# Layer-norm statistics of the feed-forward tiles moved from VectorE to two ScalarE passes, and one GpSimd instruction moved up

## The chip, the cores and the metric

The kernel runs on one core of one Trainium2 chip. The metric is device time in microseconds (us) of the whole program, the median of three runs. TensorE does the matmuls, VectorE (DVE), ScalarE (ACT) and GpSimd (POOL) the rest of the arithmetic, and SyncE (SP) issues the DMAs. Each engine runs its own queue in order; semaphores order the queues against each other.

## What is computed

A macaron block on x of 8 x 1024 rows of 256 columns: half a feed-forward, attention, half a feed-forward. The feed-forward quantizes its input and its hidden layer to four-bit values in blocks of 16:

```python
def fp4_quant_dequant(x):          # along the last axis, blocks of 16
    scale = jnp.maximum(jnp.max(jnp.abs(xb), axis=-1, keepdims=True) / 6.0, 1e-12)
    xn = xb / scale
    idx = jnp.searchsorted(_MID, jnp.abs(xn))
    q = _GRID[idx] * jnp.sign(xn) * scale

def ffn(x, w_gate, w_up, w_down):  # 256 -> 704 -> 256, each product on quantized operands
    h = silu(fp4_linear(x, w_gate)) * fp4_linear(x, w_up)
    return fp4_linear(h, w_down)

x = x + 0.5 * ffn(layernorm(x)); x = x + attention(layernorm(x)); x = x + 0.5 * ffn(layernorm(x))
```

The change touches the two layer norms ahead of the feed-forwards: mean and variance of each row of 256, then z = (x - mean) * rstd.

## The kernel before

All of x stays in SBUF as `xs`, 64 tiles of 128 rows x 256. `feed_forward(phase, ...)` runs twice, for phase 0 and 1, over the 64 tiles, one tile a step. It is a software pipeline written out by hand: each engine has a function `step(i, par)`, and `steps()` calls it for i from -6 to 63; the calls from 4 to 57 are a hardware loop of nine rounds of six steps, the others are written out. In step i an engine works on several tiles at different stages, and its queue is the order of the lines in `step`. A call `done(engine, name, i)` makes the engine wait until tile i of the named result is ready.

The stages of one tile, with the line of the profile: VectorE takes the statistics (`bn_stats` L712, `bn_aggr` L770); GpSimd makes eps_var (L824), rstd (L827) and shift = -mean * rstd (L786); ScalarE makes z (L919); VectorE takes the block maxima of z (L730) and of h (L735); GpSimd makes both scales, dscale (L840) and nscale (L851), for both at once; VectorE takes the reciprocal rec (L756); GpSimd multiplies z and h by it (v_z L793, v_h L857); ScalarE takes magnitudes (L907, L869) and VectorE rounds (L741, L675, L762, L681); GpSimd scales back (xq L818, hq L802). TensorE transposes xq (L987), ScalarE rounds the transposed tile to its high part (xT_hi L874) and VectorE makes the low part (xT_lo L704); the gate and up projections (L935) follow, then silu on ScalarE (L896) and the product h on VectorE (L720). For the hidden layer TensorE transposes hq (L951), ScalarE makes hT_hi (L880), VectorE hT_lo (L665), TensorE projects down (L942 to L945), and VectorE adds the result to `xs` (L670).

Orders within step i that matter here:

- TensorE: first bank of gate and up of tile i; transposes of tile i+1 (L987); the other banks; down projection of tile i-3, which waits for hT_lo; transposes of hq of tile i-2.
- ScalarE: silu; magnitude of v_h; magnitude of v_z; z of tile i+5, which waits for shift; xT_hi of tile i+2, which waits for the transposes; hT_hi of tile i-2.
- VectorE: hT_lo of i-3; bn_stats of i+6; h of i; the maxima; rounding; rec; rounding; xT_lo; bn_aggr of i+6.
- GpSimd: hq of i-2; xq of i+2; eps_var and rstd of i+5; dscale; shift of i+5; v_z of i+4, which waits for rec; nscale; v_h of i.

In the first steps weight preparation (`begin=weight_prep`, phase 0) or the output projection of the attention (`output_projection`, phase 1) runs between the steps, in parts, in the same queues. In the last six steps of a phase `ok(i + 6)` is false, so they issue no statistics, and the last five no z.

## Time and profile before

| | |
|---|---|
| median of three runs | 2042.45 us (2039.82 to 2044.85) |
| the profiled execution | 2039.79 us, its span 2038.0 us |
| busy share of the span | TensorE 97%, VectorE 90%, ScalarE 66%, GpSimd 53% |
| from 200 to 400 us (first feed-forward), busy of 200 us | TensorE 200.00, VectorE 196.52, ScalarE 101.25, GpSimd 175.85 |
| from 60 to 470 us | TensorE 405.86, VectorE 398.60, ScalarE 204.44, GpSimd 355.19 of 410 us |
| from 1612 to 2014 us | TensorE 402.00, VectorE 389.10, ScalarE 203.34, GpSimd 347.97 of 402 us |
| mean of one bn_stats (L712) and one bn_aggr (L770), 150 to 350 us | 0.417 us, 0.172 us |
| granted TensorE clock | 0.997 over the span, 1.00 in the feed-forwards |

The two feed-forwards take the first 480 us and the last 470 us; between them lies the attention, which the change leaves alone. The busy time of an engine is the sum of its instructions' records, overlaps counted once. Records of matmuls overlap, so a TensorE that is shown busy all the time may still lose time between the starts of its matmuls: the starts are what to read. VectorE, ScalarE and GpSimd rows show where an instruction began, how long it took, and in brackets how long its engine was idle before it and what ended that.

### The profile page before, as it was taken

To read this page: it belongs to the slowest core of one execution; us is meant where nothing else is said; L and a number is where in the kernel's file an instruction comes from. 1 tells how busy PE (TensorE), PEld (TensorE's weight loads), DVE (VectorE), ACT (ScalarE), POOL (GpSimd) and SP (SyncE) were. 2 spreads that over 40 slices of the span, in tenths; PEclk is the share of its full clock that TensorE was granted. 3 is DMA by queue.
4 is the path that set the end of the run, shared out by engine and by line. 5 is a ranking of instruction groups with operands and counts; after the bars stand their busy time and mean duration, and the time that the engine had idled before them with its cause. 6 is when DMAs were issued, how large, how long until landed. Compare 5 with 4: busy or idle time off the path is not lost. (4 is left out here: it accounts for less than half of the span.)

```text
span 2038.0 us, 44334 instructions
## 1 busy us (share of the span) xinstructions
PE 1974.5 (97%) x13254; PEld 1301.3 (64%) x13254; DVE 1838.7 (90%) x4649; ACT 1342.5 (66%) x2324; POOL 1088.6 (53%) x1785
## 2 busy tenths in 40 slices
PE   5999999998999999999999999999988899999999
PEld 3888888887887333333333333333328788888888
DVE  7999999998788899999999999999927799999997
ACT  5455555554887788888888888888883355545453
POOL 5788888885664222222222222212222688888885
PEclk9999999999999999999999999999999999999999
DMA  6000000001876555555555555555335000000000
GB/s 213 18 0 0 0 0 0 0 0 37 266 229 213 135 149 143 133 139 136 139 139 144 149 144 130 137 136 140 99 114 181 6 21 19 17 21 21 15 21 27
DMA packets 134842, 185.03 MB, mean 91 GB/s; under 512 B 24928, under 2 KB 76512, under 8 KB 134368
## 3 DMA queue, kind: packets, MB, share of 16 engines
q1 hardware_dynamic: 132000, 182.11, 31.8%
q8 instruction: 74, 1.21, 0.2%
q10 hardware_dynamic: 2688, 1.05, 0.2%
q14 instruction: 80, 0.66, 0.1%
HBM read 113.90 MB, written 85.98 MB: 98 GB/s over the span
## 5 line engine op out<-in xcount | busy, mean ns | idle before, releaser
L1939 POOL TENSOR_SCALAR_AFFINE_SELECT diag_scores<-diag_scores 128x256 f32<-128x256 f32 (+1 forms) x320 | 148.3, 463 | 672.8 <-ACT diag_scores L1908 664.9
L1404 DVE CUSTOM_DVE_ANT_0 gu_ps<-gu_ps,mask_qk 128x256 f32<-128x256 f32 (+3 forms) x690 | 340.5, 529 | 48.0 <-PE gu_ps L1389 40.3
L1389 PE MATMUL gu_ps<-k_stack,q_stack 96*128 96x512 bf16 (+3 forms) x1050 | 317.4, 334 | 2.7 <-DVE part_max L1409 0.5
L1843 PE MATMUL gu_ps<-probs,v_group 128*17 128x512 f32 (+3 forms) x3072 | 310.8, 492 | 3.2 <-ACT probs L1914 2.0
L935 PE MATMUL gu_ps<-wguT_hi,ffn_xT_hi 128*128 128x512 f32 (+1 forms) x768 | 309.1, 403 | 1.2 <-DVE ffn_xT_lo L704 1.2
L919 ACT ACTIVATE ffn_z<-xs,ffn_shift,ffn_rstd 128x256 f32 (+1 forms) x128 | 76.9, 601 | 321.7 <-POOL ffn_shift L786 321.6
L935 PE MATMUL gu_ps<-wguT_hi,ffn_xT_lo 128*128 128x512 f32 (+1 forms) x768 | 287.5, 374 | 0.0
L935 PE MATMUL gu_ps<-wguT_lo,ffn_xT_hi 128*128 128x512 f32 (+1 forms) x768 | 287.5, 374 | 0.0
L1910 ACT ACTIVATE probs<-hT_ps 128x256 f32<-128x256 f32 (+2 forms) x320 | 259.6, 811 | 13.7 <-PE hT_ps L1819 13.5
L1910 ACT ACTIVATE probs<-av_ps 128x256 f32<-128x256 f32 (+2 forms) x320 | 263.6, 824 | 0.1
L1389 PEld LDWEIGHTS gu_ps<-k_stack,q_stack 96*128 96x128 bf16 x1050 | 95.4, 97 | 256.0 <-DVE part_max L1404 183.3
L1409 DVE TENSOR_REDUCE part_max<-gu_ps 128x1 f32<-128x512 f32 x360 | 235.3, 683 | 4.3 <-PE gu_ps L1389 1.1
L1819 PE MATMUL hT_ps<-q_stack,k_stack 98*128 98x512 bf16 (+3 forms) x768 | 228.3, 327 | 2.6 <-DMA k_stack<-k_parts 2.1
L802 POOL TENSOR_TENSOR ffn_hq<-ffn_g_h,ffn_nscale 128x704 f32<-128x704 f32 (+1 forms) x256 | 210.4, 843 | 6.4 <-PE hT_ps L951 3.3
L1819 PE MATMUL av_ps<-q_stack,k_stack 98*128 98x512 bf16 (+3 forms) x768 | 191.0, 325 | 2.1 <-ACT probs L1910 1.9
L942 PE MATMUL xd_ps<-wdT_hi,ffn_hT_hi 128*128 128x256 f32 x630 | 186.2, 296 | 3.9 <-DVE ffn_hT_lo L665 3.9
L857 POOL TENSOR_TENSOR q_stack<-k_stack,ffn_rec 128x704 f32<-128x704 f32 x128 | 178.3, 1393 | 15.9 <-DVE ffn_rec L756 6.5
L942 PE MATMUL xd_ps<-wdT_hi,ffn_hT_lo 128*128 128x256 f32 x630 | 176.1, 280 | 0.0
L942 PE MATMUL xd_ps<-wdT_lo,ffn_hT_hi 128*128 128x256 f32 x630 | 176.0, 279 | 0.0
L1404 DVE CUSTOM_DVE_ANT_0 xd_ps<-xd_ps,mask_qk 128x128 f32<-128x128 f32 (+3 forms) x334 | 154.9, 493 | 6.1 <-PE xd_ps L1389 5.6
L935 PEld LDWEIGHTS gu_ps<-wguT_hi,ffn_xT_lo 128*128 128x128 f32 x768 | 144.1, 188 | 22.9
L935 PEld LDWEIGHTS gu_ps<-wguT_hi,ffn_xT_hi 128*128 128x128 f32 x768 | 144.6, 188 | 19.7 <-DVE ffn_xT_lo L704 1.9
(221 smaller groups left out, 4900.7 us busy)
## 6 DMA issues: line engine op xcount, KB each, us to landing
q_stack<-q_parts SPq DMA_DIRECT2D x192, 128.0 KB, 3.4
k_stack<-k_parts SPq DMA_DIRECT2D x192, 128.0 KB, 3.6
o_all<-o_sb SPq DMA_DIRECT2D x64, 256.0 KB
q_parts<-qkv_parts SPq DMA_DIRECT2D x32, 384.0 KB, 3.2
k_parts<-qkv_parts SPq DMA_DIRECT2D x32, 384.0 KB, 4.2
v_ones<-qkv_vst SPq DMA_DIRECT2D x16, 544.0 KB, 3.9
v_group<-v_ones SPq DMA_DIRECT2D x32, 272.0 KB, 4.3
xs<-in_L_attn_x SPq DMA_DIRECT2D x8, 1024.0 KB, 8.9
```

Of the source, the lines that this page charges most:

```text
L802: last = G.tensor_tensor(blocks(hq[:, to:to + n]), blocks(g_h[:, of:of + n]), spread(nscale[:, par, of // BLK:(of + n) // BLK]), ALU.mult)
L857: G.tensor_tensor(blocks(v_h[:, par, :]), blocks(h[:]), spread(rec[:, OF_H]), ALU.mult).then_inc(s["v_h"], 1)
L919: S.activation(z[:, 1 - par, :], x_tile(i + 5), ACT.Identity, bias=shift[:], scale=rstd[:]).then_inc(s["z"], 1)
L935: last = T.matmul(gu_ps[:, n, 0:cols.stop - cols.start], x[:, buf, k * P:(k + 1) * P], w[:, k, cols], start=k == 0 and m == 0, stop=k == K ...
L942: T.matmul(to, x[:, k * P:(k + 1) * P], w[:, k, :], start=k == 0 and n == 0, stop=False)
L1389: mm = T.matmul(out[:, e, :], qs[0:STACK, h0 + e, t * P:(t + 1) * P], ks[0:STACK, h0 + e, c * CHUNK:c * CHUNK + w], start=True, stop=True)
L1404: last = V.tensor_tensor_reduce(out=ps[:, e * w:(e + 1) * w], in0=ps[:, e * w:(e + 1) * w], in1=mask_qk[:, CHUNK - w:CHUNK], scale=1.0, sc ...
L1409: last = V.tensor_reduce(part_max[:, h0:h0 + per, t, c], ps[:, 0:per * w].rearrange("p (h w) -> p h w", h=per), AX.X, ALU.max)
L1819: mm = T.matmul(scores[pair][:, e, at:at + w], ks[0:STACK_MAX, h, t * P:(t + 1) * P], qs[0:STACK_MAX, h, (j + 1) * CHUNK - w:(j + 1) * CHUNK],
L1843: mm = T.matmul(o_ps[h * VPAD:h * VPAD + VCOLS, CHUNK - w:CHUNK], vs[:, t, h, :], probs[:, h // 2, i % 2, h % 2, at:at + w], start=first, ...
L1910: S.activation(probs[:, pair, i % 2, :, first:w], scores[pair][:, :, first:w], ACT.Exp, scale=DH ** -0.5).then_inc(s[pr], 1)
L1939: G.affine_select(out=block_of, in_=block_of, compare_op=ALU.is_ge, fill=MASKED, base=0, pattern=[[0, 2], [0, count], [1, P]], channel_mul ...
```

## The change

The statistics leave VectorE. `bn_stats` and `bn_aggr` go. ScalarE takes, for each tile, a copy with a summed output (`summed`, tile i+7 in step i) and a square of (x - mean) with a summed output (`squared`, tile i+6); both stand ahead of z of tile i+5. Their full outputs go to unused scratch columns. GpSimd gets one more instruction a step, `averaged`, which makes -mean of tile i+6 from the sum; eps_var becomes a multiply and an add on immediates, and shift a product of two columns. GpSimd's nscale is moved ahead of v_z. The written-out steps reach to 7 and start again at 56, so the loop has eight rounds in place of nine. ScalarE instead of VectorE waits for the loads of x and, in the output projection, for the finished rows.

```diff
@@ -540,6 +540,7 @@
...
                     S.activation(next_table[:, :], minus_half[:, :], ACT.Silu)
+                out_done(act, "resid", 2 if part < OUT_PARTS - 1 else OUT_CHUNKS - 1)
@@ -569,7 +570,7 @@
...
-        names = ("stats aggr eps rstd shift z amax_z amax_h dscale nscale rec v_h v_z av_h av_z u_h u_z g_h g_z hq xq "
+        names = ("total mean squares eps rstd shift z amax_z amax_h dscale nscale rec v_h v_z av_h av_z u_h u_z g_h g_z hq xq "
                  "xT xT_hi xT_lo gate up silu h hT hT_hi hT_lo down resid stored").split()
@@ -589,8 +590,8 @@
...
-                stats, aggr, eps_var, rstd, shift = (tmp("stats", [P, 6]), tmp("aggr", [P, 2]), tmp("eps_var", [P, 1]),
-                                                     tmp("rstd", [P, 1]), tmp("shift", [P, 1]))
+                total, squares, eps_var, rstd, shift = (tmp(n, [P, 1]) for n in ("total", "squares", "eps_var", "rstd", "shift"))
+                minus_mean = tmp("minus_mean", [P, 2])
                 xq = tmp("xq", [P, DIM])
@@ -613,6 +614,8 @@
...
+                scratch = [m[:, GROUP - 1, SEQ - DIM:SEQ] for m in second_stacks]
                 GU_BANKS = [slice(a, min(a + CHUNK, 2 * HIDDEN)) for a in range(0, 2 * HIDDEN, CHUNK)]
@@ -631,13 +634,17 @@
...
+                def first_step(i):
+                    return isinstance(i, int) and i == -AHEAD
                 def early(i, first=1):
...
-                    first, last, unroll = 4, TILES - 6, 6
+                    first, last, unroll = 8, TILES - 8, 6
                     for i in range(-AHEAD, first):
@@ -707,9 +714,6 @@
...
                                 hT_low(i - 3, hT, hT_flat)
-                            if ok(i + 6):
-                                done(dve, "aggr", i + 5)
-                                V.bn_stats(stats[:], x_tile(i + 6)).then_inc(s["stats"], 1)
                             if phase == 0 and early(i) and i == 1:
@@ -761,30 +765,25 @@
...
                                                        op0=ALU.max, op1=ALU.subtract).then_inc(s["g_z"], 1)
-                            if ok(i + 6):
-                                done(dve, "stats", i + 6)
-                                done(dve, "shift", i + 5)
                             if ok(i + 2) and not (early(i, -2) and i == -2):
                                 xT_low(i + 2, par)
-                            if ok(i + 6):
-                                V.bn_aggr(aggr[:], stats[:]).then_inc(s["aggr"], 1)
-                        def other_batches(i):
-                            if i is None:
-                                for b in range(2, BATCH):
-                                    dve.wait_ge(x_loaded[b], 16)
-                            elif (i + AHEAD) % SEQ_TILES == 0:
-                                dve.wait_ge(x_loaded[(i + AHEAD) // SEQ_TILES], 16)
-                        steps("vector", dve, step, finish, other_batches if phase == 0 else None)
+                        steps("vector", dve, step, finish)
...
                     def _(pool):
-                        def shifted(i):
+                        def shifted(i, par):
                             done(pool, "rstd", i)
                             pool.nop(nofuse=True)
-                            G.tensor_scalar(shift[:], aggr[:, 0:1], rstd[:], -1.0, ALU.mult,
-                                            ALU.mult).then_inc(s["shift"], 1)
+                            G.tensor_tensor(shift[:], minus_mean[:, par:par + 1], rstd[:], ALU.mult).then_inc(s["shift"], 1)
+                        def averaged(i, par):
+                            done(pool, "total", i)
+                            done(pool, "shift", i - 2)
+                            done(pool, "squares", i - 2)
+                            pool.nop(nofuse=True)
+                            G.tensor_scalar(minus_mean[:, par:par + 1], total[:], -1.0 / DIM, 0.0, ALU.mult,
+                                            ALU.add).then_inc(s["mean"], 1)
@@ -817,17 +816,22 @@
...
                                                 ALU.mult).then_inc(s["xq"], 1)
+                            if first_step(i):
+                                averaged(0, par)
+                            if ok(i + 6) and not first_step(i):
+                                averaged(i + 6, par)
                             if ok(i + 5):
-                                done(pool, "aggr", i + 5)
+                                done(pool, "squares", i + 5)
                                 done(pool, "z", i + 4)
-                                G.tensor_tensor(eps_var[:], aggr[:, 1:2], eps_tile[:, 0:1],
+                                pool.nop(nofuse=True)
+                                G.tensor_scalar(eps_var[:], squares[:], 1.0 / DIM, EPS, ALU.mult,
                                                 ALU.add).then_inc(s["eps"], 1)
...
                             if early(i, 0):
-                                shifted(i + 5)
+                                shifted(i + 5, 1 - par)
                             if early(i):
@@ -840,9 +844,7 @@
...
                             if ok(i + 5) and not early(i, 0):
-                                shifted(i + 5)
-                            if ok(i + 4) and not early(i, 0):
-                                over_scale_z(i, par)
+                                shifted(i + 5, 1 - par)
                             if ok(i) or ok(i + 4):
@@ -850,6 +852,8 @@
...
                                                 ALU.mult, ALU.min).then_inc(s["nscale"], 1)
+                            if ok(i + 4) and not early(i, 0):
+                                over_scale_z(i, par)
                             if ok(i):
@@ -884,6 +888,18 @@
...
                             S.copy(hT_end[0][:], hT_end_ps).then_inc(s["hT_hi"], 1)
+                        def summed(i):
+                            done(act, "mean", i - 1)
+                            act.nop(nofuse=True)
+                            S.activation(scratch[0], x_tile(i), ACT.Copy, accum_out=total[:]).then_inc(s["total"], 1)
+                        def squared(i, par):
+                            done(act, "mean", i)
+                            done(act, "eps", i - 1)
+                            act.nop(nofuse=True)
+                            S.activation(scratch[1], x_tile(i), ACT.Square, bias=minus_mean[:, par:par + 1],
+                                         accum_out=squares[:]).then_inc(s["squares"], 1)
@@ -912,10 +928,17 @@
...
                                 xT_high(0, par)
+                            if first_step(i):
+                                summed(0)
+                            if ok(i + 6):
+                                squared(i + 6, par)
+                            if ok(i + 7):
+                                summed(i + 7)
                             if ok(i + 5):
...
                                 done(act, "shift", i + 5)
+                                act.nop(nofuse=True)
                                 S.activation(z[:, 1 - par, :], x_tile(i + 5), ACT.Identity, bias=shift[:],
@@ -924,7 +947,16 @@
...
-                        steps("scalar", act, step, finish)
+                        def other_batches(i):
+                            if i is None:
+                                for b in range(1, BATCH):
+                                    act.wait_ge(x_loaded[b], 16)
+                            elif i == -AHEAD:
+                                act.wait_ge(x_loaded[0], 16)
+                            elif (i + AHEAD + 1) % SEQ_TILES == 0:
+                                act.wait_ge(x_loaded[(i + AHEAD + 1) // SEQ_TILES], 16)
+                        steps("scalar", act, step, finish, other_batches if phase == 0 else None)
```

## Rows read from the trace of the kernel before

**Rows 1.** Timeline of TensorE, one step: start us, us, line, output<-inputs, [idle before <-releaser]
```profile
256.43 0.38 PE L987 MATMUL xd_ps<-ident,ffn_xq 128*128 128x128 f32 x2
...
259.12 0.36 PE L942 MATMUL xd_ps<-wdT_hi,ffn_hT_hi 128*128 128x256 f32 x1
259.31 0.28 PE L942 MATMUL xd_ps<-wdT_lo,ffn_hT_hi 128*128 128x256 f32 x1
...
263.24 0.38 PE L987 MATMUL xd_ps<-ident,ffn_xq 128*128 128x128 f32 x2
```
**Rows 2.** Timelines of ScalarE and VectorE in the same step
```profile
256.35 0.60 ACT L919 ACTIVATE ffn_z<-xs,ffn_shift,ffn_rstd 128x256 f32 x1 [2.77 <-POOL ffn_shift L786]
256.90 0.37 ACT L874 CAST ffn_xT_hi<-xd_ps 128x256 fp32r<-128x256 f32 x1
257.17 0.81 ACT L880 CAST ffn_hT_hi<-hT_ps 128x768 fp32r<-128x768 f32 x1
...
257.76 0.17 DVE L770 BATCH_NORM_AGGREGATE ffn_aggr<-ffn_stats 128x2 f32<-128x6 f32 x1
258.01 0.96 DVE L665 TENSOR_TENSOR ffn_hT_lo<-hT_ps,ffn_hT_hi 128x768 fp32r<-128x768 f32 x1
```
**Rows 3.** Second feed-forward's last steps, which issue no statistics: TensorE, VectorE, ScalarE
```profile
1983.32 0.38 PE L987 MATMUL xd_ps<-ident,ffn_xq 128*128 128x128 f32 x2
...
2010.57 0.38 PE L987 MATMUL xd_ps<-ident,ffn_xq 128*128 128x128 f32 x2
...
1991.71 0.96 DVE L665 TENSOR_TENSOR ffn_hT_lo<-hT_ps,ffn_hT_hi 128x768 fp32r<-128x768 f32 x1 [0.17 <-ACT ffn_hT_hi L880]
...
1997.42 0.37 ACT L874 CAST ffn_xT_hi<-xd_ps 128x256 fp32r<-128x256 f32 x1 [3.35 <-PE xd_ps L987]
```
**Rows 4.** Timeline of TensorE at the last tile but one: down projection begins
```profile
2019.86 0.28 PE L942 MATMUL xd_ps<-wdT_hi,ffn_hT_hi 128*128 128x256 f32 x1
2019.97 0.28 PE L942 MATMUL xd_ps<-wdT_lo,ffn_hT_hi 128*128 128x256 f32 x1
```
**Rows 5.** Timeline of GpSimd over one step
```profile
257.29 0.42 POOL L851 TENSOR_SCALAR ffn_nscale<-ffn_amax 128x60 f32<-128x60 f32 x1
257.79 1.39 POOL L857 TENSOR_TENSOR q_stack<-k_stack,ffn_rec 128x704 f32<-128x704 f32 x1
...
260.74 0.62 POOL L818 TENSOR_TENSOR ffn_xq<-k_stack,ffn_nscale 128x256 f32<-128x256 f32 x1
261.32 0.19 POOL L824 TENSOR_TENSOR ffn_eps_var<-ffn_aggr,eps_tile 128x1 f32<-128x1 f32 x1
261.59 0.56 POOL L827 TENSOR_TENSOR ffn_rstd<-ffn_eps_var,minus_half 128x1 f32<-128x1 f32 x1
262.24 0.42 POOL L840 TENSOR_SCALAR ffn_dscale<-ffn_amax 128x60 f32<-128x60 f32 x1
262.75 0.27 POOL L786 TENSOR_SCALAR ffn_shift<-ffn_aggr,ffn_rstd 128x1 f32<-128x1 f32 x1
263.39 0.62 POOL L793 TENSOR_TENSOR q_stack<-ffn_z,ffn_rec 128x256 f32<-128x256 f32 x1 [0.37 <-DVE ffn_rec L756]
```
**Rows 6.** GpSimd in the ramp, v_h then v_z; L840's narrow form over the span (mean ns)
```profile
49.78 1.39 POOL L857 TENSOR_TENSOR q_stack<-k_stack,ffn_rec 128x704 f32<-128x704 f32 x1
51.13 0.62 POOL L793 TENSOR_TENSOR q_stack<-ffn_z,ffn_rec 128x256 f32<-128x256 f32 x1
...
L840 POOL TENSOR_SCALAR ffn_dscale<-ffn_amax 128x16 f32<-128x16 f32 x7 | 1.9, 274 | 16.9 <-DVE ffn_amax L730 16.9
```
**Rows 7.** ScalarE groups: a 4-column activation and a function table load (busy us, mean ns)
```profile
L429 ACT ACTIVATE w_first_table<-minus_half 128x4 f32<-128x4 f32 x1 | 0.2, 205 | 0.0
L429 ACT ACT_TABLE_LOAD x1 | 1.3, 1283 | 0.7 <-PEq L2008 0.7
```
**Rows 8.** First ramp: stretch, length, busy us (x instructions) of PE, PEld, DVE, ACT, POOL; VectorE's next row
```profile
22.00:37.00 15.00, 12.24 (x52) 8.57 (x53) 13.57 (x27) 13.36 (x28) 8.03 (x16) 1.00 0.63 187
...
37.06 0.69 DVE L306 SCALAR_TENSOR_TENSOR qkv_z<-hT_ps,q_stack 128x512 f32<-128x512 f32 x1 [0.51 <-ACT hT_ps L405]
```

## The prediction, made before the change was run

> **What bounds the kernel now.** The table of busy times by stretch comes first: over both feed-forwards TensorE is shown busy without a gap, VectorE 98%, GpSimd 88% and ScalarE half of the time. That doesn't say which of them sets the step, so I went on to the timelines of one step on every engine. A step is the distance between two transposes of xq: 263.24 - 256.43 = 6.81 us [rows 1]. Nearly every step of both phases takes that, and about one in six, where the loops turn, 0.03 more.
>
> TensorE can't run this step much faster, and it isn't alone in its loop. Follow the transposes: they end at 256.43 + 0.38 = 256.81; xT_hi starts at 256.90 and hT_hi, next in ScalarE's queue, at 257.17; that ends at 257.98 and hT_lo starts at 258.01; that ends at 258.97 and the down projection starts at 259.12 [rows 1, 2]. From there TensorE runs through to its next transposes. So one closed chain, transposes, xT_hi, hT_hi, hT_lo, down projection, holds the whole step, and the only loss of TensorE's in it is at the down projection: its first two matmuls start 0.19 us apart [rows 1], where at the one place at which hT_lo had long been ready they start 0.11 apart [rows 4]. Together with a gap of some 0.03 in front of them that is about 0.1 us a step.
>
> Three other things are nearly as long as the step. z, which waits 2.77 us for shift, starts at 256.35 and takes 0.60, so it ends just about when xT_hi starts [rows 2]. VectorE's queue is full. GpSimd waits for rec for only 0.37 us a step [rows 5].
>
> **What leaves VectorE.** bn_stats, right behind hT_lo (0.42 us by the table of busy times), and bn_aggr, right in front of it (0.17) [rows 2], go: some 0.6 us of VectorE's step. Is any of it on the closed chain? hT_lo follows the end of hT_hi by 0.03 us [rows 2], so neither bn_aggr in front of it nor bn_stats behind it holds it. The trace has the experiment in it: the last steps of the second phase issue no statistics. There VectorE sits idle for 0.17 us before hT_lo, and ScalarE, with no z to make, sits idle for 3.35 us before xT_hi and is released by the transposes all the same; yet four steps take 2010.57 - 1983.32 = 27.25 us, 6.81 each [rows 3]. VectorE's relief is worth nothing in the steady steps but the 0.03 us at a turn of the loop: eight turns a phase instead of nine, and less lateness at each, together under 1 us of the program. I count it at 0.5 us.
>
> **What comes to GpSimd.** This is the term that decides. Its queue has 0.37 us of wait, of which 0.08 would stay as the gap after a small instruction: 0.29 us is free [rows 5]. nscale ahead of v_z fills the wait for rec with work, so all of it can be used. The additions, from start to start: xq is followed 0.04 before its end by eps_var (261.32 against 260.74 + 0.62), but `averaged` carries a no-op that holds its waits, as dscale does behind rstd, where the gap is +0.09 (262.24 against 261.59 + 0.56): +0.13. `averaged` itself is a tensor-scalar on one column. No row shows one with two immediates; L840 takes 0.42 at 60 columns [rows 5] and 0.274 at 16 [rows 6], which is 0.0033 a column and 0.226 at one, and shift, at one column with a column operand, took 0.27 [rows 5]. I take 0.226, since it is the same form of instruction as L840, and keep 0.27 as the upper end. The gap to eps_var: +0.09. eps_var as tensor-scalar instead of tensor-tensor: 0.226 - 0.19 = +0.04. shift as a tensor-tensor like eps_var: 0.19 - 0.27 = -0.08. The new order saves gaps: today 0.08 (after shift), 0.09 (ahead of nscale), 0.08 (nscale to v_h, 257.79 against 257.71) [rows 5]; afterwards 0.09, 0.08 and, between v_z and v_h, both tensor-tensor without a no-op, -0.04, as between the two at 51.13 against 49.78 + 1.39 [rows 6]: -0.12. Sum: 0.13 + 0.226 + 0.09 + 0.04 - 0.08 - 0.12 = 0.28 us, into 0.29 free. GpSimd's own step becomes 6.81 - 0.29 + 0.28 = **6.80 us**, a hair under 6.81. With 0.27 for both tensor-scalars it is 6.89; if v_z and v_h don't overlap either, 7.01; a low end with a little cheaper instructions is 6.75, which is worth nothing since 6.81 stays.
>
> **What comes to ScalarE.** Per step two passes over 128x256 ahead of z. Their window: counted from v_z (263.39 - 6.81 = 256.58), v_h starts at 257.16, hq at 258.51, xq at 260.11, `averaged` at 260.82 and ends at 261.05; the square may start at 261.18. In the same count shift ends at 262.79 (now 263.02), so z could start at 262.92, 0.2 earlier than now, and it delays xT_hi only if it starts after about 263.2. The window is 1.7 us to the first, 2.0 to the second. The price: a copy like xT_hi, 0.37; the square between that and z's 0.60 [rows 2]; reading out each sum, which no row shows, between nothing and 0.205, the smallest activation [rows 7]. Two passes come to 0.8 to 1.4 us, and the likeliest value is 1.3, since the read-out is likely an instruction of its own, with its gaps. That fits; the cover is the wait for shift of 2.77 us [rows 2], of which 1.4 or so is used after its wait for the mean. Queued behind the new wait for the mean are the copy, z, xT_hi and hT_hi, and TensorE waits for the last two; but shift comes from the same queue later than the mean does, so the wait for the mean alone ends nothing last.
>
> The Trainium skill ("ScalarE: Activation LUTs", section on what a table load costs) prices an activation at 186 ns + 0.833 ns an element with 93 ns for each column operand: 0.40 and 0.49 us here, 0.89 for the pair without read-outs. z, with two such operands, is 0.585 by it and 0.60 in the row, so it agrees; the sum would be the same. The same page (section on table sets) says that cheap functions sit in every set; it doesn't name the square among the fillers, and no row here shows Square beside Silu.
>
> **The ramps.** In phase 0 ScalarE is full from 22 to 37 us, 13.36 of 15, with the weights' casts, and VectorE waits 0.51 us for it right behind [rows 8]. Three steps fall in it, each with two more passes: 3 x 1.3 = 3.9 us less the statistics VectorE no longer takes; part of it is taken up in ScalarE's later idle. I take +3 us, with 0 and +5 as ends. In phase 1 no such full stretch stands in the ramp, so I take 0, with -1 and +1 as ends. The waits for the loads of x and for the finished rows move from one queue to another behind work that needed them anyway: 0.
>
> **Sum.** 2039.8 (profiled execution) + 3 + 0 - 0.5 + 0 = 2042.3. That execution lies 2.7 us under the median of the runs, so against the median it is 2042.45 + 2.5, say **2045 us**.
>
> **Rivals.** (a) GpSimd sets the step. If its queue sums to more than 6.81, nothing covers it: TensorE waits. The statistics' instructions are there in about 54 steps a phase, 108 in all. At 6.89 that is 0.08 x 108 = 9 us, at 7.01 22 us; typical 12 us, 2057 us. For it: 0.01 us of room and one instruction form that no row shows. Against it: each gap I used repeats in every step. It decides from 0.02 us a step on.
>
> (b) ScalarE's passes don't fit: over 1.0 us each, z comes late, then hT_hi and the down projection. At 1.2 each, 0.4 late less about 0.15 of slack, some 0.25 x 108 = 27 us, 2072 us. A table load of 1.283 us [rows 7] on each change between Square and Silu would be far worse: two a step add 2.6 us, past the window by over 1.5, 160 us or more. Against it: Abs, Identity and Silu follow each other in every step now without a load.
>
> (c) VectorE is what holds the step, through the turns of the loop, and its relief lets hT_lo come early enough that TensorE's 0.1 us at the down projection goes: -0.11 x 118 = -13 us, 2032 us with the ramp. For it: VectorE's 98%. Against it: the steps without statistics [rows 3].
>
> (d) The change does what it says but the moved nscale brings nothing: then GpSimd's wait for rec stays beside the additions, which is (a) at its upper end.
>
> **Chances.** Forecast (step stays 6.81) 0.55; (a) with (d) 0.27; (b) 0.09; (c) 0.09. About 0.3%, 6 us, is what a measurement of this kernel can tell from no change. (c) is the faster case: 0.09. (a) and (b) are slower: some of (a) falls under 6 us at its low end, and the forecast goes over it with the ramp at its high end; these even out: 0.27 + 0.09 = 0.36. Same: 0.55. The range leaves out (b) and (c), with 0.18: from 2037 (no ramp cost and the scatter of the runs, 2.5 us either way) to 2063 ((a) at three quarters of its upper end).
>
> **What would show it.** Right: transposes still 6.81 apart; hT_lo 0.03 behind hT_hi with VectorE idle before it and before h, some 0.2 and 0.4 us; GpSimd without a wait worth naming; ScalarE's wait before z down from 2.77 to about 1 in two parts, one ahead of the square for the mean. (a): GpSimd without any gap, transposes 6.85 or more apart, TensorE waiting for hT_lo longer. (b): no wait in front of z and xT_hi starting later than 0.1 after the transposes. (c): transposes 6.7 apart and the first two matmuls of the down projection 0.11. `averaged` over 0.25 us, or a sum's read-out over 0.4, makes the prediction wrong.

## The result and the profile after

The changed kernel takes 2045.61 us in the median (2042.15 to 2048.24), the kernel before 2041.8 us (2039.18 to 2044.85) on the same chips: 1.0019 times, with a 95% interval of 1.0012 to 1.0025. So it is slower by 3.8 us, 0.2%. The forecast was 2045.0 us, in its case "the step stays 6.81".

| | before | after |
|---|---|---|
| median, us | 2041.8 | 2045.61 |
| span of the profiled execution, us | 2038.0 | 2044.8 |
| mean step in the first / second feed-forward, us | 6.813 / 6.817 | 6.821 / 6.834 |
| fifth transposes of xq in the first feed-forward start at, us | 61.25 | 65.23 |

The mean steps are from transposes to transposes over the loops' stretch. The two spans differ by 6.8 us, where the medians differ by 3.8: one profiled execution is only one execution. Where it is looked for in the spans, 4.0 us have come in by the fifth transposes; in the steps, 0.008 and 0.017 us each, some 1.5 us in 118.

The rest of the 6.8 us isn't the change's. Between the fifth and the sixth transposes 12.81 us pass after and 11.27 before: TensorE waits 2.46 us for xT_lo in both, and at the end of this wait the clock granted to the changed kernel is 0.50, the 1.2 GHz level, from 70.4 to 73.8 us, where the kernel before keeps 1.00. The experiments below show that this fall comes with either ramp: e4, e6 and e9, without passes on ScalarE in the first one, have it, and e5, e8 and e12, with them, don't. In the second ramp it is the other way round: the kernel before is granted 0.50 from 1608.1 to 1611.5 us, and the changed kernel keeps 1.00, which gives 1.5 us back. A last 1.4 us stands in the attention, which the change leaves alone.

First the stretches, after (stretch, length, busy us and instructions of PE, PEld, DVE, ACT, POOL; clock; DMA):

```profile
22.00:37.00 15.00, 9.89 (x39) 6.80 (x40) 12.28 (x20) 12.63 (x30) 9.33 (x18) 0.98 0.49 149
200.00:400.00 200.00, 200.00 (x1259) 177.82 (x1258) 183.82 (x325) 129.04 (x293) 179.77 (x324) 1.00 0.00 0
```

and the second stretch before:

```profile
200.00:400.00 200.00, 200.00 (x1263) 178.28 (x1262) 196.52 (x383) 101.25 (x175) 175.85 (x296) 1.00 0.00 0
```

In the steady stretch the change does what it says: VectorE goes from 98% to 92%, ScalarE from 51% to 65%, GpSimd from 88% to 90%, and TensorE stays without a gap. So work has moved off a nearly full engine, and the step hasn't moved. The loss shows in the ramp: TensorE does 9.89 us in the 15 us where it did 12.24 [rows 8].

One step after, on ScalarE and VectorE (start us, us, engine, line, output<-inputs, [idle before <-releaser]); it answers to [rows 2]:

```profile
253.48 0.51 ACT L901 ACTIVATE k_stack<-xs,ffn_minus_mean 128x256 bf16 x1 [1.35 <-POOL ffn_eps_var L828]
253.90 0.19 ACT L901 ACTIVATION_READ_ACCUMULATOR k_stack<-xs,ffn_minus_mean 128x1 f32 x1
253.99 0.40 ACT L895 ACTIVATE q_stack<-xs 128x256 bf16 x1
254.30 0.18 ACT L895 ACTIVATION_READ_ACCUMULATOR q_stack<-xs 128x1 f32 x1
254.90 0.60 ACT L942 ACTIVATE ffn_z<-xs,ffn_shift,ffn_rstd 128x256 f32 x1 [0.42 <-issue]
255.82 0.37 ACT L878 CAST ffn_xT_hi<-xd_ps 128x256 fp32r<-128x256 f32 x1 [0.32 <-PE xd_ps L1019]
256.09 0.81 ACT L884 CAST ffn_hT_hi<-hT_ps 128x768 fp32r<-128x768 f32 x1
...
256.93 0.96 DVE L672 TENSOR_TENSOR ffn_hT_lo<-hT_ps,ffn_hT_hi 128x768 fp32r<-128x768 f32 x1 [0.17 <-ACT ffn_hT_hi L884]
...
258.26 0.89 DVE L724 TENSOR_TENSOR k_stack<-k_stack,gu_ps 128x704 f32<-128x704 f32 x1 [0.37 <-PE gu_ps L967]
```

Both passes and their two read-outs stand in ScalarE's old wait for shift; of its 2.77 us 1.35 is left ahead of the square, and z starts 0.45 us ahead of the transposes at 255.35, where it started 0.08 ahead of them before. hT_lo follows the end of hT_hi by 0.03 us, as it did, only that VectorE now sits idle for 0.17 us before it. What ends the wait ahead of the square is eps_var and not the mean: the square writes `squares` anew, which eps_var of the tile before still has to read (`done(act, "eps", i - 1)`), and it starts 0.08 after eps_var's end (253.21 + 0.19).

GpSimd in the same step, which answers to [rows 5]:

```profile
252.94 0.19 POOL L785 TENSOR_SCALAR ffn_minus_mean<-ffn_total 128x1 f32<-128x1 f32 x1
253.21 0.19 POOL L828 TENSOR_SCALAR ffn_eps_var<-ffn_squares 128x1 f32<-128x1 f32 x1
253.48 0.56 POOL L831 TENSOR_TENSOR ffn_rstd<-ffn_eps_var,minus_half 128x1 f32<-128x1 f32 x1
254.13 0.42 POOL L844 TENSOR_SCALAR ffn_dscale<-ffn_amax 128x60 f32<-128x60 f32 x1
254.63 0.19 POOL L778 TENSOR_TENSOR ffn_shift<-ffn_minus_mean,ffn_rstd 128x1 f32<-128x1 f32 x1
254.90 0.42 POOL L853 TENSOR_SCALAR ffn_nscale<-ffn_amax 128x60 f32<-128x60 f32 x1
255.51 0.63 POOL L792 TENSOR_TENSOR q_stack<-ffn_z,ffn_rec 128x256 f32<-128x256 f32 x1 [0.19 <-DVE ffn_rec L760]
256.09 1.39 POOL L861 TENSOR_TENSOR q_stack<-k_stack,ffn_rec 128x704 f32<-128x704 f32 x1
```

The wait for rec has shrunk from 0.37 to 0.19, and it isn't gone: GpSimd isn't the bound.

### The profile page after: what moved, and what is told of

It reads as the page before. It is cut to its first block and busy times, and to the rows that moved or that the text cites. A ratio compares the mean times of both kernels' runs of the same rounds, so it can differ in the third digit from the quotient of the medians.

```text
span 2044.8 us, 45026 instructions
## 1 busy us (share of the span) xinstructions
PE 1977.6 (97%) x13254; PEld 1304.7 (64%) x13254; DVE 1782.6 (87%) x4393; ACT 1459.3 (71%) x2836; POOL 1107.5 (54%) x1913
## 5 line engine op out<-in xcount | busy, mean ns | idle before, releaser
L901 ACT ACTIVATE k_stack<-xs,ffn_minus_mean 128x256 bf16 (+1 forms) x128 | 65.1, 508 | 152.2 <-POOL ffn_eps_var L828 149.2
L724 DVE TENSOR_TENSOR k_stack<-k_stack,gu_ps 128x704 f32<-128x704 f32 x128 | 113.6, 887 | 51.9 <-PE gu_ps L967 46.4
```

The source lines that it names most:

```text
L724: V.tensor_tensor(h[:], silu[:], up_ps, ALU.mult).then_inc(s["h"], 1)
```

## The experiments

Times are medians; the ratio is to the kernel before in runs on the same chip, with its 95% interval. "First" and "second" are the mean steps of the two feed-forwards in the profiled execution, and "fifth" is when the fifth transposes of xq in the first feed-forward start: with two passes on ScalarE or without, it tells what the ramp has cost by then. e11, an addition on GpSimd over 60 columns of f32, has no time, since its tile left too little room in SBUF for the others; e12, over 32 columns in bf16, took its place.

| kernel | us | ratio [95%] | first | second | fifth |
|---|---|---|---|---|---|
| before | 2041.8 | 1 | 6.813 | 6.817 | 61.25 |
| after | 2045.61 | 1.0019 [1.0012, 1.0025] | 6.821 | 6.834 | 65.23 |
| e1 before, hT_hi first | 2035.54 | 0.9966 [0.9952, 0.9979] | 6.782 | 6.736 | 61.23 |
| e2 after, hT_hi first | 2032.43 | 0.9948 [0.9934, 0.9961] | 6.714 | 6.739 | 64.97 |
| e3 after, nscale moved back | 2077.63 | 1.0173 [1.0159, 1.0187] | 7.187 | 7.128 | 64.05 |
| e4 before, narrow statistics | 2040.22 | 0.9993 [0.9984, 1.0002] | 6.811 | 6.815 | 60.86 |
| e5 after, one more on GpSimd | 2045.41 | 1.0014 [1.0005, 1.0024] | 6.853 | 6.851 | 64.15 |
| e6 change in second only | 2042.26 | 0.9997 [0.9988, 1.0006] | 6.814 | 6.834 | 61.43 |
| e7 change in first only | 2046.08 | 1.0024 [1.0011, 1.0037] | 6.806 | 6.816 | 63.90 |
| e8 before, passes in the ramp | 2047.12 | 1.0024 [1.0015, 1.0034] | 6.833 | 6.833 | 65.10 |
| e9 before, nscale moved | 2039.88 | 0.9992 [0.9983, 1.0001] | 6.810 | 6.814 | 61.39 |
| e10 e2, ramp's statistics on VectorE | 2026.24 | 0.9930 [0.9916, 0.9943] | 6.734 | 6.694 | 61.50 |
| e12 after, a wider one on GpSimd | 2050.14 | 1.0048 [1.0031, 1.0064] | 6.878 | 6.874 | 65.14 |

**Is VectorE's relief worth anything as the kernel stands (e4)?** The kernel before with bn_stats over 16 columns instead of 256; it leaves the other 240 out of the mean and the variance, so its results are not those of the block:

```diff
-V.bn_stats(stats[:], x_tile(i + 6)).then_inc(s["stats"], 1)
+V.bn_stats(stats[:], x_tile(i + 6)[:, 0:BLK]).then_inc(s["stats"], 1)
```

> The kernel before with bn_stats over 16 of the 256 columns, so the statistics are of a part of each row: the read cost is taken from VectorE and nothing is added elsewhere. Theory of the closed chain: VectorE's relief of about 0.25 us a step is worth nothing but the turns of the loop, 0 to 1 us, 2041 to 2042. Rival (VectorE sets the step): 0.1 x 118 = 12 us faster, about 2030.

bn_stats falls from a mean of 417 ns to 167 ns in every step, and the steps stay 6.811 and 6.815. The time is the same within the interval. That is 0.25 us of the 0.6 that the change takes from VectorE; with all of it gone, the changed kernel's steps are 6.82 and 6.83. Rival (c) of the prediction, VectorE as what holds the step, falls.

**Is the closed chain what holds it (e1, e2)?** ScalarE's hT_hi needs only the six transposes of hq, which are done early; it stands behind xT_hi in the queue. Both kernels issue it ahead of z instead, e1 in the kernel before, e2 in the changed one (the lines are e1's; e2 has the same two under its passes):

```diff
+if ok(i - 2) and not early(i, 2):
+    hT_high(i - 2)
 if ok(i + 5):
...
     xT_high(i + 2, par)
-if ok(i - 2) and not early(i, 2):
-    hT_high(i - 2)
```

> The kernel before, with one move in ScalarE's queue: hT_hi of tile i-2 ahead of z of tile i+5, into the wait for shift, so that it no longer stands behind the transposes of xq. Theory of the closed chain (transposes, xT_hi, hT_hi, hT_lo, down projection): the chain is cut, but VectorE's own queue, 6.78 us a step, holds hT_lo at nearly the same time as now, so at most 0.03 x 118 = 3.5 us faster, 2038 to 2042. Rival, that the matmuls alone make 6.81 us: no change in the step. If VectorE were not full after all: 0.1 x 118 = 12 us faster.

> The changed kernel with the same move: hT_hi of tile i-2 between the two statistics passes and z. Theory of the closed chain: VectorE has room now, so hT_lo follows xT_lo at once, about 0.26 us earlier than in the changed kernel, TensorE's first two matmuls of the down projection start 0.11 us apart and not 0.19, and the step falls from 6.82 to about 6.70: 0.11 x 116 = 13 us faster than the changed kernel, about 2033. Rival, that the matmuls alone make the step: 2045, as the changed kernel. Rival, that z comes too late behind hT_hi: xT_hi late by up to 0.1 us, but nothing waits for it then; 2045.

One step of e2, on ScalarE, TensorE and VectorE:

```profile
258.63 0.78 ACT L884 CAST ffn_hT_hi<-hT_ps 128x768 fp32r<-128x768 f32 x1
259.30 0.38 PE L1019 MATMUL xd_ps<-ident,ffn_xq 128*128 128x128 f32 x2
259.31 0.60 ACT L944 ACTIVATE ffn_z<-xs,ffn_shift,ffn_rstd 128x256 f32 x1
259.81 0.35 ACT L878 CAST ffn_xT_hi<-xd_ps 128x256 fp32r<-128x256 f32 x1
260.41 0.41 DVE L711 TENSOR_TENSOR ffn_xT_lo<-xd_ps,ffn_xT_hi 128x256 fp32r<-128x256 f32 x1
260.74 0.95 DVE L672 TENSOR_TENSOR ffn_hT_lo<-hT_ps,ffn_hT_hi 128x768 fp32r<-128x768 f32 x1
261.96 0.28 PE L974 MATMUL xd_ps<-wdT_hi,ffn_hT_hi 128*128 128x256 f32 x1
262.07 0.28 PE L974 MATMUL xd_ps<-wdT_lo,ffn_hT_hi 128*128 128x256 f32 x1
...
266.03 0.38 PE L1019 MATMUL xd_ps<-ident,ffn_xq 128*128 128x128 f32 x2
```

hT_hi is over before xT_hi starts, hT_lo follows xT_lo without a wait and is done 0.27 us before the down projection, whose first two matmuls are 0.11 us apart, as at [rows 4]. The step is 6.73 here, 6.71 and 6.74 in the mean. So the chain held it, and TensorE's 0.1 us came back when it was cut. GpSimd has no wait left in the first feed-forward of e2: 0.08 us ahead of v_z, and v_z follows v_z after 6.71, which is what GpSimd's own queue takes (the part on the prediction works it out). So with the chain cut GpSimd's queue is as long as the step. e1 gains 6.4 us, where I had expected at most 3.5 from it, and 12 if VectorE weren't full; the same step there:

```profile
257.08 0.17 DVE L770 BATCH_NORM_AGGREGATE ffn_aggr<-ffn_stats 128x2 f32<-128x6 f32 x1
257.17 0.92 DVE L665 TENSOR_TENSOR ffn_hT_lo<-hT_ps,ffn_hT_hi 128x768 fp32r<-128x768 f32 x1
...
258.24 0.36 PE L942 MATMUL xd_ps<-wdT_hi,ffn_hT_hi 128*128 128x256 f32 x1
258.44 0.28 PE L942 MATMUL xd_ps<-wdT_lo,ffn_hT_hi 128*128 128x256 f32 x1
...
258.64 0.89 DVE L720 TENSOR_TENSOR k_stack<-k_stack,gu_ps 128x704 f32<-128x704 f32 x1 [0.21 <-POOL q_stack L857]
```

VectorE still idles ahead of h there, so its queue isn't the bound even with the statistics in it. But hT_lo, behind bn_aggr, ends only 0.15 before the down projection, and the two matmuls stay 0.20 apart. In the first feed-forward the relief of VectorE is therefore worth 6.782 - 6.714 = 0.07 us a step once the chain is cut. In the second the steps are equal (6.736 and 6.739), but they are made up differently: the first two matmuls are 0.144 us apart in the mean in e1 and 0.121 in e2, and e2 loses the difference again between the second matmul and the next transposes (the last section has these spacings). In the medians e2 is 3.1 us below e1, but their intervals overlap and e2's five runs lie between 2028.67 and 2036.39; by the profiled executions its steps gain some 4 us over e1 and its ramp costs as much. Which of the two kernels is faster isn't shown.

**Is GpSimd near its bound (e3, e9, e5, e12)?** e3 is the changed kernel with nscale back behind v_z; e9 is the kernel before with nscale moved ahead of v_z and nothing else (the lines are e3's, and e9's are their reverse):

```diff
+if ok(i + 4) and not early(i, 0):
+    over_scale_z(i, par)
 if ok(i) or ok(i + 4):
...   (nscale)
-if ok(i + 4) and not early(i, 0):
-    over_scale_z(i, par)
```

> The changed kernel with nscale back behind v_z. Theory that GpSimd's queue is full: its own work is 6.75 us a step, and the wait for rec, with nothing to fill it, comes on top. From dscale's end to v_z are rec's 0.52 us and two hand-overs of 0.05 and 0.14, of which shift and its gap cover 0.28: 0.35 us uncovered (plus 0.05 of gaps that the move saved). GpSimd then needs 6.75 + 0.4 = about 7.1 us a step, so 0.3 x 108 = 30 us slower than the changed kernel, about 2075. Rival, that GpSimd has room and the move is without effect: 2045.

> The kernel before with nscale moved ahead of v_z and nothing else. Theory that the move only makes room in GpSimd's queue, and that the queue had 0.29 us of room already: no change, 2041 to 2043. Rival, that an earlier v_h (and so an earlier magnitude and rounding) shortens the step: 2 to 8 us faster.

e3's GpSimd; the second row is one step behind the first:

```profile
256.33 0.63 POOL L792 TENSOR_TENSOR q_stack<-ffn_z,ffn_rec 128x256 f32<-128x256 f32 x1 [0.43 <-DVE ffn_rec L760]
257.04 0.42 POOL L855 TENSOR_SCALAR ffn_nscale<-ffn_amax 128x60 f32<-128x60 f32 x1
...
263.52 0.63 POOL L792 TENSOR_TENSOR q_stack<-ffn_z,ffn_rec 128x256 f32<-128x256 f32 x1 [0.43 <-DVE ffn_rec L760]
```

263.52 - 256.33 = 7.19, and the wait for rec stands beside the additions: rivals (a) and (d) together, 36 us. e9 is the same as the kernel before; its wait for rec only grows from 0.37 to 0.52, since the reordered queue is 0.15 shorter. The move is worth nothing alone, and the change can't do without it.

e5 and e12 add one independent tensor-scalar ahead of the mean in the loops of the changed kernel, on one column and on 32:

```diff
...
+pool.nop(nofuse=True)
+G.tensor_scalar(spare[:], minus_half[:, 0:1], 1.0 / DIM, 0.0, ALU.mult, ALU.add)
```

> The changed kernel with one more one-column tensor-scalar on GpSimd in each of the 96 steps of the loops, 0.19 + 0.09 = 0.28 us with its gap. GpSimd's own step was 6.75 us, so 0.06 to 0.07 us of room. Theory that GpSimd's queue sets the step as soon as it is full: step 7.03, 0.21 x 96 = 20 us slower than the changed kernel, about 2066. Rival, that GpSimd's lateness is absorbed elsewhere in the pipeline: 2045 to 2050.

> The changed kernel with one more tensor-scalar over 32 columns on GpSimd in each of the 96 steps of the loops. The one-column instruction lengthened GpSimd's queue by 0.15 us of start to start, since it overlapped its neighbour; 32 columns take about 0.14 us more (60 columns take 0.42, one takes 0.19). Theory that GpSimd sets the step once full: its own step is 6.75 + 0.15 + 0.12 = 7.0, so 0.18 x 96 = 17 us slower than the changed kernel, about 2062. Rival, that its lateness is absorbed in the pipeline: 2046 to 2050.

The addition in e5, then in e12, with the instruction behind it, and v_z one step apart:

```profile
254.00 0.62 POOL L793 TENSOR_TENSOR q_stack<-ffn_z,ffn_rec 128x256 f32<-128x256 f32 x1
...
258.24 0.19 POOL L822 TENSOR_SCALAR ffn_spare<-minus_half 128x1 f32<-128x1 f32 x1
258.39 0.19 POOL L786 TENSOR_SCALAR ffn_minus_mean<-ffn_total 128x1 f32<-128x1 f32 x1
...
260.86 0.62 POOL L793 TENSOR_TENSOR q_stack<-ffn_z,ffn_rec 128x256 f32<-128x256 f32 x1
```

```profile
252.86 0.22 POOL L822 TENSOR_SCALAR ffn_spare<-ident 128x32 bf16<-128x32 f32 x1
253.03 0.19 POOL L786 TENSOR_SCALAR ffn_minus_mean<-ffn_total 128x1 f32<-128x1 f32 x1
...
255.50 0.62 POOL L793 TENSOR_TENSOR q_stack<-ffn_z,ffn_rec 128x256 f32<-128x256 f32 x1
...
262.39 0.62 POOL L793 TENSOR_TENSOR q_stack<-ffn_z,ffn_rec 128x256 f32<-128x256 f32 x1
```

The wait for rec is gone in both, GpSimd is packed, and the steps are 6.85 and 6.88. So GpSimd does set the step once its own queue passes it (6.86 and 6.89 from v_z to v_z). On the mechanism I was right, on the size not: I expected 2066 and 2062 us, and 2045.41 and 2050.14 came, which by themselves would fit the rival that the lateness is absorbed (2045 or 2046 to 2050) as well. It is the rows above that decide. The one-column operation costs 0.15 us from start to start and not 0.28, since it overlaps the next by 0.04 instead of standing a gap ahead of it. e5's time doesn't show the 0.03 us a step (some 3 us in all): it is 3.0 us over the kernel before, the changed kernel 3.8. e12's does: 8.9 us over it, 5.1 more than the changed kernel, where 0.05 us a step over 108 steps make 5.4.

**Where do the 3.8 us sit (e6, e7, e8, e10)?** e6 has the change in the second feed-forward alone, e7 in the first alone, each by calling the other kernel's function for the other one. e8 is the kernel before with two passes on ScalarE ahead of z in the first eight steps of the first feed-forward, whose sums nobody reads:

```diff
...
+for n in range(2):
+    if i > -AHEAD:
+        act.wait_ge(s["spare"], 2 * (i + AHEAD) + n - 1)
+    act.nop(nofuse=True)
+    S.activation(scratch[n], x_tile(i + 6), ACT.Copy, accum_out=spare[:, n:n + 1]).then_inc(s["spare"], 1)
```

> The kernel before in the first feed-forward and the changed one in the second. Theory that the added time is the first ramp (transposes of tile 10 at 98.47 us instead of 92.99): the first part is as before, and the second ramp gave back 1.5 us in the one profile, so 2040 to 2043. Rival, that the steady steps cost the added time (6.83 instead of 6.81 in the second phase): 2043 to 2046.

> The changed kernel in the first feed-forward and the one before in the second. Theory that the added time is the first ramp: 2041.8 + 4 to 5.5, 2045 to 2047. Rival (steady steps of the second phase): 2042 to 2043.

> The kernel before with two copies with a summed output added on ScalarE ahead of z in the first eight steps of the first feed-forward only; nobody reads them, and VectorE keeps its statistics. Theory that the ramp's cost is ScalarE's queue, full from 22 to 37 us: the same delay as in the changed kernel, 3 to 5.5 us slower than before, 2045 to 2047. Rival, that it is the longer chain of waits from sum to mean to squares: 2041 to 2043.

The second feed-forward's share is -0.1 us within ±1.8, the first's +3.7, and the passes alone, in the ramp alone, make at least as much, 4.8 us; so it isn't the longer chain from sum to mean to squares, which e8 hasn't got. Some 2 us of e8's 4.8 may not be the ramp, though: its profiled execution has 6.833 in both feed-forwards, 0.016 to 0.020 a step over the kernel before with the same code in those steps. The fifth transposes tell the same: with passes on ScalarE seven kernels have them between 63.90 and 65.23 (64.65 in the mean), without them six have them between 60.86 and 61.50 (61.28). The difference is 3.4 us. How it comes, before and then after, in ScalarE's queue:

```profile
21.87 0.60 ACT L405 ACTIVATE hT_ps<-k_stack 128x512 fp32r<-128x512 f32 x1 [2.43 <-DVE k_stack L309]
22.41 0.58 ACT L919 ACTIVATE ffn_z<-xs,ffn_shift,ffn_rstd 128x256 f32<-128x256 f32 x1
22.90 1.05 ACT L410 CAST wqkvT_hi<-gu_ps 128x512 fp32r<-128x512 f32 x2
```

```profile
22.50 0.60 ACT L405 ACTIVATE hT_ps<-k_stack 128x512 fp32r<-128x512 f32 x1 [3.41 <-DVE k_stack L309]
23.04 0.49 ACT L901 ACTIVATE k_stack<-xs,ffn_minus_mean 128x256 bf16<-128x256 f32 x1
23.43 0.19 ACT L901 ACTIVATION_READ_ACCUMULATOR k_stack<-xs,ffn_minus_mean 128x1 f32 x1
23.53 0.40 ACT L895 ACTIVATE q_stack<-xs 128x256 bf16<-128x256 f32 x1
23.83 0.18 ACT L895 ACTIVATION_READ_ACCUMULATOR q_stack<-xs 128x1 f32 x1
23.93 0.58 ACT L942 ACTIVATE ffn_z<-xs,ffn_shift,ffn_rstd 128x256 f32<-128x256 f32 x1
24.42 1.04 ACT L410 CAST wqkvT_hi<-gu_ps 128x512 fp32r<-128x512 f32 x2
```

0.63 us are lost by the first row, and the pair in front of z adds 0.89: the weights' casts, on which TensorE waits, start 1.52 us later. A further pair at 32.37 adds 0.90, which makes 2.4 us. TensorE's next matmul that waits for these casts is 2.39 us late, before and then after:

```profile
31.99 0.51 PE L361 MATMUL gu_ps<-wguT_hi,neg_ident 128*128 128x512 f32 x1 [0.67 <-ACT wguT_hi L410]
```

```profile
34.38 0.51 PE L361 MATMUL gu_ps<-wguT_hi,neg_ident 128*128 128x512 f32 x1 [1.55 <-ACT wguT_hi L410]
```

The first transposes are 3.0 us late, and the last 0.6 us is the clock: after this wait of 1.55 us the changed kernel is granted 0.50, the 1.2 GHz level, from 36.3 to 39.7 us, and the kernel before 1.00 there. All seven kernels with passes in this ramp have the longer wait (1.46 to 1.55 us) and a fall to 0.50 that begins at 34.4 to 36.6 us; the six without wait 0.67 us and keep 1.00. So the fall goes with the passes, and it goes on behind the first transposes: five matmuls of L146 take 2.25 us where they took 1.41. What it makes of the 3.4 us in all isn't told apart.

e10 is e2 with the statistics of the first six tiles of the first feed-forward left on VectorE, by bn_stats and bn_aggr as before, and with ScalarE's passes from the seventh tile on:

```diff
+if isinstance(i, int) and ramp(i + 6):
+    ...
+    V.bn_stats(stats[:], x_tile(i + 6)).then_inc(s["stats"], 1)
```

> The changed kernel with hT_hi ahead of z, and with the statistics of the first six tiles of the first feed-forward left on VectorE, so that ScalarE has no passes in its full stretch. Theory that ScalarE's queue is what the first ramp pays for: the ramp's 3.8 us come back, 2032.4 - 3.8 = about 2029 (2027 to 2031), 12 to 14 us faster than before. Rival, that the ramp pays for something else: 2032.

```profile
61.50 0.41 PE L1046 MATMUL xd_ps<-ident,ffn_xq 128*128 128x128 f32 x2 [0.45 <-POOL ffn_xq L840]
...
257.40 0.28 PE L1001 MATMUL xd_ps<-wdT_hi,ffn_hT_hi 128*128 128x256 f32 x1
257.52 0.28 PE L1001 MATMUL xd_ps<-wdT_lo,ffn_hT_hi 128*128 128x256 f32 x1
```

The fifth transposes are back at 61.50, the steps stay short, the granted clock stays 1.00 through the ramp, and the kernel takes 2026.24 us, 15.1 less than the kernel before in the same comparison, where e2 has 9.5: it is faster than both, and faster than the 2027 to 2031 that I had expected. Of the 5.6 us between e10 and e2, 3.5 are those of the ramp (61.50 against 64.97). The step in the second feed-forward is shorter too (6.694 against 6.739) and in the first it is longer (6.734 against 6.714); of such differences the last section says more.

## Why the prediction was right, step by step

**The closed chain: shown.** The prediction had the step stay, with hT_lo 0.03 behind hT_hi and VectorE idle before it and before h by 0.2 and 0.4 us. Measured: 6.82 and 6.83, 0.03, 0.17 and 0.37. e1 and e2 show the cause by cutting it.

**VectorE's relief worth nothing in steady steps: shown** by e4. The -0.5 us for the turns of the loop isn't seen: the steps' means are 0.008 and 0.017 us longer, not shorter. Neither difference can be put down to the change: e7 has the changed kernel's first feed-forward and takes 6.806 in it, less than before, and e8 has the second feed-forward of the kernel before and takes 6.833. What I didn't see is that the relief has a use once the chain is cut.

**GpSimd's sum: the mechanism was right, two terms were too large.** I took 0.226 us for each tensor-scalar on one column, on a line through 16 and 60 columns; both took 0.192. And the reordering saved 0.15 and not 0.12. (The terms as written add up to 0.286 and not 0.28, so the forecast's room was next to nothing.) The queue's own step was to be 6.80. It is 6.70: 6.81 from v_z to v_z less 0.11, by which the wait for rec in front (0.19) is longer than the gap behind a small instruction (0.08). e5's packed queue says the same: 260.86 - 254.00 - 0.15 = 6.71. The two terms make up the difference (0.034 + 0.034 + 0.03). So there was 0.11 us of room and not 0.01, and rival (a) with (d), at a chance of 0.27, was further off than I thought. (Three quarters of its upper end on top of 2045 is 2061.5, not the 2063 that stands as the end of the range.) Its mechanism exists: e3, e5 and e12 show it.

**ScalarE's two passes: the size was a little too large.** I took 1.3 us for the pair, between 0.8 and 1.4. From the square's start to the end of the second read-out it is 254.48 - 253.48 = 1.00 us: 0.42 to the read-out, 0.09 to the copy, 0.31, and 0.18. I was right that the read-out is an instruction of its own; but it starts 0.09 before the record of its pass ends, and the copy starts 0.10 before that of the read-out ends. One wait I had wrong: the square was to follow the mean, and it follows eps_var, 0.27 us later; the window of 1.7 us was in truth 1.4, and it still held the pair. Of ScalarE's wait 1.35 and 0.42 us are left in two parts, 1.8 and not about 1. There is no table load between Square, Copy, Identity and Silu (the whole execution has three, at 0.7, 501.7 and 1577.9 us), and z isn't late: rival (b) falls with both of its forms.

The Trainium skill ("ScalarE: Activation LUTs", section on what a table load costs) has 186 ns for an activation, 0.833 ns an element and 93 ns for each column operand, by which the two passes would be an estimated 0.49 and 0.40 us. The rows have 0.51 and 0.40, so the trace agrees.

**The ramp: right in place, 3 us against 3.4** by the fifth transposes. I had counted three steps at 1.3, of which some would be taken up later; it is two full pairs in the stretch of [rows 8], at 0.89 and 0.90 up to the next instruction, and 0.63 us from the pairs before it, 2.4 together, and then a granted clock of 0.50 for 3.4 us, for which the prediction had no term. That 3 came out so near is in part luck: pairs counted too dear stood in for the clock. The second ramp, put at 0, is 0 within 1.8 us (e6, which measures the second feed-forward as a whole).

**The sum** was 2039.8 + 2.5 against the profiled execution and 2045 against the median: the median moved by 3.8 and not 2.5. Most of it is the ramp, by the fifth transposes and by e6 and e7. How the 3.8 us divide between the ramp and steps that are a hundredth longer stays open: the intervals of e6 and e7 are 2 to 3 us wide either way. Against the forecast's 2045 the median is 0.6 us off, because the median of the kernel before came out 0.65 lower (2041.8 and not 2042.45) while the effect came out 1.3 larger.

## What to carry to other kernels

An engine at 98% whose instruction nobody waits for isn't the bound: relief is worth what the closed chain of the step allows, and here the next gain was one cast ahead in ScalarE's queue, on which 0.1 us a step of TensorE hung. With that cast moved, the engine that took the work over, GpSimd, had no wait left. The trace's own steps without the moved work are the cheapest experiment there is. Passes that are free in a loop, in the shadow of a wait, are paid in full in a ramp where the same engine is full, and TensorE's longer wait there can cost it its clock as well: move the steady part, and leave the ramp's where it was.

## What the runs showed of the hardware

**A packed GpSimd queue.** A tensor-scalar with two immediates on one column is 0.192 us, on 32 columns (f32 to bf16) 0.22. What it costs from start to start depends on what is around it. The mean, which signals a semaphore and has a no-op behind it, takes 0.27 (253.21 - 252.94). The added operation of e5 and e12, which signals nothing, takes 0.15 and 0.17, though the mean's no-op is behind it. That the missing signal makes the difference was argued from these rows and not tried.

**An operand just in time costs TensorE more than its wait.** The first two matmuls of the down projection, neither of which reads hT_lo, are 0.19 to 0.20 us apart where hT_lo ends 0.15 us before them (before, after, e1's first feed-forward), and 0.11 to 0.12 where it ends 0.27 or 0.30 before (e2, e10: 262.07 - 261.96 and 257.52 - 257.40).

**TensorE's clock and its waits in the ramp.** In the first ramp thirteen profiled executions, one of each kernel, fall into two groups: seven in which TensorE waits 1.46 to 1.55 us for the weights' casts, and the granted clock is 0.50 for 3.4 us a little later, and six in which it waits 0.67 us and keeps 1.00. At the end of the later wait of 2.44 to 2.46 us, ahead of the sixth transposes, the clock falls in seven of the thirteen, with passes or without (after, e2, e3, e4, e6, e7, e9), and each time it costs some 1.5 us (12.81 and 11.27 us from the fifth transposes to the sixth). So the same wait doesn't always bring the fall.

**Matmul spacing that differs where the code is the same.** The rest of the down projection, from its second matmul to the transposes behind it (16 spacings), is 1.87 us in the mean of the kernel before's second feed-forward, 1.91 in after's and e2's and 1.85 in e10's. It isn't the statistics: e8, whose code of the second feed-forward is that of the kernel before, has 1.91 too. Not all of it reaches the step: in e8 half comes back before the next transposes, and the step is 0.016 us longer (6.833 against 6.817). But e2 and e10, with the same code in the second feed-forward, have 6.739 and 6.694, and over 59 steps 0.045 us is 2.7 us, nearly as much as the effect that was measured here. Each kernel has one profiled execution, so whether it goes with the program or with the execution isn't shown, and what sets it, I haven't found.
